# Local attention inside a four-stage kernel: weights scaled on VectorE and turned by transposes, small products spread over more steps

## The reference

```
g  = groupnorm(x)                       (groups of 3 channels over all pixels)
l  = layernorm(g) over the 96 channels of a pixel, times lg, plus lb
n  = g scaled to unit length over the 96 channels of a pixel
for each pixel q, over the keys k with |dy| <= 7 and |dx| <= 7 inside the image:
    s[k]  = n[q] . n[k]                 (-1e9 outside the window)
    w     = softmax over the 8 largest s[k], 0 elsewhere
    a[q]  = sum of w[k] * g[k]
t  = l + a
out = x + t + w2 relu(w1 t + b1) + b2
```

## Time and profile before

| | us |
|---|---|
| median of 3 runs | 18,090.14 |
| the profiled execution | 18,087.81 |
| its span | 18,086.0 |
| busy: TensorE, VectorE, ScalarE, GpSimd | 14,292.3, 15,507.5, 11,827.0, 12,383.2 |
| stage `local`: first to last instruction | 10719 to 11677 |
| its loop over tiles | 10820.5 to 11661.6 |
| TensorE's mean granted clock, whole span | 0.906 |

### The profile page before, as it was taken

One profiled execution on the slowest core, in us unless ns is written; L12 is line 12 of the kernel. 1 busy time (PEld: TensorE's weight loads), 2 busy tenths in 40 slices (PEclk: granted clock), 3 DMA queues, 4 the chain that ended last, 5 costly groups with the idle time before them and its releaser, 6 DMA issues. The chain is left out here.

```text
span 18086.0 us, 184332 instructions
## 1 busy us (share of the span) xinstructions
PE 14292.3 (79%) x38972; PEld 5918.2 (33%) x38972; DVE 15507.5 (86%) x20601; ACT 11827.0 (65%) x24107; POOL 12383.2 (68%) x5929
## 2 busy tenths in 40 slices
PE   7998878888888868888888868767777767777776
PEld 2222233333333323333333325423333233333333
DVE  6666489999999979999999964489999958999996
ACT  3555556667777636767677734378888827888882
POOL 0000079999999939999999941179988806998881
PEclk9999899999999989999999977788888888888888
DMA  1000033333333323333333321122222212222220
GB/s 27 13 18 11 12 93 107 106 107 107 107 107 106 102 77 106 108 106 107 107 106 107 106 78 37 37 67 81 82 79 79 78 29 72 81 81 79 79 80 29
DMA packets 542714, 1404.62 MB, mean 78 GB/s; under 512 B 135503, under 2 KB 191863, under 8 KB 538599
## 3 DMA queue, kind: packets, MB, share of 16 engines
q1 hardware_dynamic: 541586, 1392.84, 27.0%
HBM read 1311.24 MB, written 58.30 MB: 76 GB/s over the span
## 5 line engine op out<-in xcount | busy, mean ns | idle before, releaser
L996 PE MATMUL PS<-Hc,ident 128*128 128x448 f32 x16128 | 7494.1, 598 | 1950.8 <-POOL Hc L1308 1596.6
L1300 POOL TENSOR_TENSOR Tr<-du,BC 128x1344 f32<-128x1344 f32 x2688 | 8161.1, 3036 | 60.7 <-DVE du L1179 60.5
L996 PEld LDWEIGHTS PS<-Hc,ident 128*128 128x128 f32 x16128 | 3106.2, 205 | 6212.5 <-POOL Hc L1308 2579.3
L1118 ACT ACTIVATE PS<-dl,A 128x448 f32<-128x448 f32 x5376 | 3403.3, 633 | 2049.9 <-DVE Hr L1226 1248.6
L1308 POOL TENSOR_TENSOR Hc<-Hr,BC 128x448 f32<-128x448 f32 (+1 forms) x2688 | 3892.6, 1448 | 1030.1 <-DVE Hr L1226 947.2
L1226 DVE TENSOR_TENSOR_SCAN PS<-PS,st,Tr 128x448 f32<-128x448 f32 x3072 | 3358.2, 1135 | 142.8 <-ACT st L1132 140.6
L1233 DVE TENSOR_TENSOR Hc<-PS,BC 128x448 f32<-128x448 f32 x4480 | 2564.0, 605 | 0.0
L1126 ACT ACTIVATE PS<-cs,lneps,A 128x448 f32<-128x448 f32 x2688 | 1941.0, 722 | 175.2 <-DVE PS L1226 171.6
L719 POOL MEMSET pad<- 128x348 f32 x6 | 2.3, 387 | 2800.6 <-POOLq L67 2800.6
L1209 DVE SCALAR_TENSOR_TENSOR PS<-PS,Tr 128x448 f32<-128x448 f32 x2688 | 1644.2, 612 | 225.0 <-ACT PS L1126 214.0
L1118 ACT ACTIVATE Ar<-dl,A 128x448 f32<-128x448 f32 x2688 | 1765.5, 657 | 0.0
(11 more groups left out here) (254 smaller groups left out, 16125.1 us busy)
## 6 DMA issues: line engine op xcount, KB each, us to landing
BC<-bcscratch SPq DMA_DIRECT2D x5376, 224.0 KB, 3.6
zscratch<-zst SPq DMA_DIRECT2D x84, 224.0 KB, 2.0
bcscratch<-rows SPq DMA_DIRECT2D x336, 56.0 KB, 2.9
z<-zscratch SPq DMA_DIRECT2D x28, 672.0 KB, 4.5
xg<-mid SPq DMA_DIRECT2D x12, 1176.0 KB, 8.3
xr<-mid SPq DMA_DIRECT2D x56, 168.0 KB, 2.6
rl<-rows SPq DMA_DIRECT2D x56, 168.0 KB, 3.5
Q<-part SPq DMA_DIRECT2D x72, 98.0 KB, 4.4
```

The lines of the kernel that those rows point to most:

```text
L996: e.matmul(PS[:, YB + c, 0:T], K["ident"][:], Hc[:, g % NHC, c, :], start=False, stop=(nn == 15)).then_inc(y_done, 1)
L1118: e.activation(decay_at(u), dl[:, q % 2, c, :], ACT.Exp, scale=A[:, q // NT, c, nn:nn + 1]).then_inc(a_done, 1)
L1300: e.tensor_tensor(Tr[:, g % NTR], du[:, q % 2], b, ALU.mult).then_inc(t_done, 1)
```

## The change

In the stage `local` only:

- The diagonal matrix and ScalarE's `diagonal` go. VectorE multiplies E by one over the sum (`scale`, in place, a new instruction between `negate` and the `match_replace`, which becomes `replace`), and `turn` on TensorE is a transpose with the identity.
- `bias` moves from the end of VectorE's step to just behind `mask_`, one step later. `output` becomes two calls, one product in each of two steps.
- The small products of the next image stand in steps 4 to 14 (before: 9 to 16), about two of three steps for each kind. Each kind has its own pair of semaphores; for image one each kind also has a bank of its own (7, 5, 6), for the others all share bank 7 as before. `mean`, `total`, `normal` and the roots fall into earlier steps.
- `add`, `query` and `similar` wait for the rows of xl and xn that they read, no longer for the whole image; for image one only two of seven `scale` calls stand ahead of the loop, the rest in its first steps.
- SP loads xg ahead of the weights, the load of the next image moves from step 0 of an image to step 26 of the one before, and `bands` to steps 11 to 14.

```diff
-CENTRE, STAT, TURN = 9, 10, 9
+KINDS = {"mean": 0, "var": 0, "centre": 0, "stat": 1, "turn": 2}
+ROOTS, SCALE = 16, 18
+
+
+def spaced(s, first, n):
+
+    return next((k for k in range(n) if first + 3 * k // 2 == s), None)
 
 
 def small_products(s):
 
-    a = {4: ("mean", 0), 5: ("var", 0)}.get(s)
-    if CENTRE <= s < CENTRE + NT:
-        a = ("centre", s - CENTRE)
-    b = ("stat", s - STAT) if STAT <= s < STAT + NT else None
-    c = ("turn", s - TURN) if TURN <= s < TURN + 6 else None
+    a = {1: ("mean", 0), 2: ("var", 0)}.get(s)
+    if spaced(s, 4, NT) is not None:
+        a = ("centre", spaced(s, 4, NT))
+    b = ("stat", spaced(s, 5, NT)) if spaced(s, 5, NT) is not None else None
+    c = ("turn", spaced(s, 4, 6)) if spaced(s, 4, 6) is not None else None
     return a, b, c
 
 
...
+        def bank(b, name):
+
+            return {0: 7, 1: 5, 2: 6}[KINDS[name]] if b == 0 else 7
...
-                e.wait_ge(b7_free, order[b, what])
+                for kind in range(3):
+                    n = ahead[b, what][kind]
+                    if n and (b or kind == KINDS[name]):
+                        e.wait_ge(small_free[kind], n)
...
+                if j == 0:
+                    e.wait_ge(xn_ready, NT * b + (ys.stop - 1) // 8 + 1)
...
-                e.wait_ge(chosen, n + 1)
-                e.wait_ge(diag, n + 1)
+                e.wait_ge(scaled, n + 1)
...
                 for h, blocks in enumerate(key_blocks(i, j)):
                     for k, (_, off, kn) in enumerate(blocks):
-                        a = e.matmul(PS[0:kn, 2 + h, 112 * k:112 * k + 112], E[:, n % 2, off:off + kn], dg[:, n % 2, :],
-                                     start=True, stop=True)
+                        a = e.transpose(PS[0:kn, 2 + h, 112 * k:112 * k + 112], E[:, n % 2, off:off + kn],
+                                        K["ident"][0:112, 0:112])
                 a.then_inc(w_turned, 1)
 
             def gather(n):
...
-            def output(g):
-                e.wait_ge(hid_ready, 2 * g + 2)
-                for h in range(2):
-                    a = e.matmul(PS[0:C, 5, 0:T], w2[:, h, :], hid[:, h, :], start=(h == 0), stop=(h == 1))
-                a.then_inc(out_mm, 1)
+            def output(g, h):
+                e.wait_ge(hid_ready, 2 * g + h + 1)
+                e.matmul(PS[0:C, 5, 0:T], w2[:, h, :], hid[:, h, :], start=(h == 0), stop=(h == 1)).then_inc(out_mm, 1)
...
-            def diagonal(n):
-                s = n % 2
-                e.wait_ge(divided, n + 1)
-                if n >= 2:
-                    e.wait_ge(w_turned, n - 1)
-                e.activation(dg[:, s, :], K["ident"][0:112, 0:112], ACT.Copy, scale=den[:, s, 1:2]).then_inc(diag, 1)
...
+            def scale(n):
+                s, nk = n % 2, size(n)
+                e.wait_ge(chosen, n + 1)
+                e.wait_ge(divided, n + 1)
+                e.tensor_scalar(E[:, s, 0:nk], E[:, s, 0:nk], den[:, s, 1:2], None, ALU.mult).then_inc(scaled, 1)
+
             def negate(n):
-                s, nk = n % 2, size(n)
+                s = n % 2
                 e.wait_ge(topped, n + 1)
                 e.tensor_scalar(nb[:, s:s + 1], m8[:, s, 0:1], -1.0, None, ALU.mult).then_inc(negated, 1)
+
+            def replace(n):
+                s, nk = n % 2, size(n)
                 if n >= 2:
                     e.wait_ge(chosen, n - 1)
                 e.match_replace(R[:, s, 0:nk], m8[:, s, :], S[:, s, 0:nk], -3e9).then_inc(replaced, 1)
...
-                if i == 0 and j == 0:
-                    e.wait_ge(xl_ready, NT * (b + 1))
+                if j == 0:
+                    e.wait_ge(xl_ready, NT * b + i + 1)
...
+                if band_step(r, 10) is not None:
+                    bias(band_step(r, 10))
                 if 0 <= r - 1 < STEPS:
                     divide(r - 1)
                 if r < STEPS:
                     top(r)
-                if more and s == 4:
+                if more and s == 1:
                     mean(b + 1)
                 if 0 <= r - 1 < STEPS:
                     choose(r - 1)
                 if r < STEPS:
                     negate(r)
+                if 0 <= r - 1 < STEPS:
+                    scale(r - 1)
+                if r < STEPS:
+                    replace(r)
                 if 0 <= r - 4 < STEPS:
                     add(r - 4)
+                if more and s == 0:
+                    total(b + 1)
                 if more and s == 3:
-                    total(b + 1)
-                if more and s == 6:
                     normal(b + 1)
-                if more and s == 18:
+                if more and s == ROOTS:
                     inverted(b + 1)
-                if band_step(r, 9) is not None:
-                    bias(band_step(r, 9))
 
         def pool(e):
             def scale(b, u):
@@ -2235,37 +2261,39 @@
 
             def query(n):
                 b, i, j = tile(n)
-                if i == 0 and j == 0:
-                    e.wait_ge(xn_ready, NT * (b + 1))
+                if j == 0:
+                    e.wait_ge(xn_ready, NT * b + i + 1)
                 if n >= 4:
                     e.wait_ge(sim, n - 3)
...
-            for u in range(NT):
+            for u in range(2):
                 scale(0, u)
             for n in range(2):
                 query(n)
-            for r in range(STEPS + 13):
+            for r in range(STEPS + 14):
                 b, s = divmod(r, NTL)
-                if b + 1 < NI and 20 <= s < 20 + NT:
-                    scale(b + 1, s - 20)
+                if r + 2 < NT:
+                    scale(0, r + 2)
+                if b + 1 < NI and SCALE <= s < SCALE + NT:
+                    scale(b + 1, s - SCALE)
                 if r + 2 < STEPS:
                     query(r + 2)
-                if band_step(r, 9) is not None:
-                    finish(band_step(r, 9))
+                if band_step(r, 10) is not None:
+                    finish(band_step(r, 10))
...
+            load(0)
             for k in W:
                 e.dma_start(W[k][:], D[k]).then_inc(w_ld, 16)
-            load(0)
             for u in range(NT):
                 row(0, u)
             fold(0)
@@ -2326,25 +2354,26 @@
             for u in range(NT):
                 spread(0, u)
             bands(0, range(4))
-            for r in range(STEPS + 14):
+            load(1)
+            for r in range(STEPS + 15):
                 b, s = divmod(r, NTL)
                 if b + 1 < NI:
-                    if s == 0:
-                        load(b + 1)
-                    if STAT <= s < STAT + NT:
-                        row(b + 1, s - STAT)
-                    if s == 17:
+                    if spaced(s, 5, NT) is not None:
+                        row(b + 1, spaced(s, 5, NT))
+                    if s in (11, 12, 13, 14):
+                        bands(b + 1, [s - 11])
+                    if s == ROOTS - 1:
                         fold(b + 1)
-                    if s == 19:
+                    if s == SCALE - 1:
                         unfold(b + 1)
-                    if 19 <= s < 19 + NT:
-                        spread(b + 1, s - 19)
-                    if s in (20, 22, 24, 26):
-                        bands(b + 1, [(s - 20) // 2])
-                if band_step(r, 4) is not None:
-                    rest(band_step(r, 4))
-                if band_step(r, 10) is not None:
-                    store(band_step(r, 10))
+                    if SCALE - 1 <= s < SCALE - 1 + NT:
+                        spread(b + 1, s - SCALE + 1)
+                if b + 2 < NI and s == 26:
+                    load(b + 2)
+                if band_step(r, 5) is not None:
+                    rest(band_step(r, 5))
+                if band_step(r, 11) is not None:
+                    store(band_step(r, 11))
             for i in range(2):
                 e.wait_ge(y_out[i], 16 * len(range(i, 7 * NI, 2)))
```

More of the change, by code:

```diff
@@ L1829, in local @@
     PS = chip.PS
-    order = {}
+    order, ahead, counts = {}, {}, [0, 0, 0]
     for b in range(NI):
@@ L1834, in local @@
                 if what:
-                    order[b, what] = len(order)
+                    kind = KINDS[what[0]]
+                    ahead[b, what] = list(counts)
+                    order[b, what] = counts[kind]
+                    counts[kind] += 1
     with ExitStack() as ctx:
@@ L1857, in local @@
         gn_dve, gn_act = sems("gn_dve"), sems("gn_act")
-        b7_full, b7_free = sems("b7_full"), sems("b7_free")
+        small_full, small_free = ([sems(f"{n}_{kind}") for kind in range(3)] for n in ("small_full", "small_free"))
         squared, st_ld, fe_ld, q_ready = sems("squared"), sems("st_ld"), sems("fe_ld"), sems("q_ready")
@@ L1871, in local, with full, free @@
         y_out = [sems("y_out") for _ in range(2)]
+        def bank(b, name):
+            return {0: 7, 1: 5, 2: 6}[KINDS[name]] if b == 0 else 7
+        def full(name):
+            return small_full[KINDS[name]]
```

(40 more changed lines are left out.)

36 lines of the change are left out of this document (18 added, 18 removed).

## The result

The changed kernel takes 18,292.5 us (median of 4 runs, 18,284.7 to 18,300.3), the kernel before, timed beside it, 18,091.6 (4 runs): ratio 1.0112, interval 1.0094 to 1.0129, or 201 us more. The forecast, 18,233, was 59 us short, inside its range. The profiled execution took 18,284.7 us with a span of 18,282.8, 196.8 more than the profiled one of before.

A forecast was written before the change was run, and what follows sets the result against it. The prediction took a loop through TensorE and VectorE, neither full, to bound the stage, with the clock level mattering most. Terms 38 + 17 - 8 + 98 = +145 us on 18,087.8 gave 18,233 us, range 18,075 to 18,320.

The forecast's parts named there:

- scaling on VectorE: New scaling of E before replace and add, on the loop: 0.34 us a step, +38 us, ends 0 and +65.
- bias moved: bias now behind mask, ahead of add, in 28 steps: +17 us, ends 0 and 19.
- start: Before step 4: 18 us saved by early xg and three banks, mostly lost behind image two's sum: -8 us, ends -20 and +5.
- small products, outputs: TensorE's small products over steps 4 to 14, output in two steps: directly 0; small products' ends -10 and +10 us.
- transposes, direct: Turn by transposes saves TensorE some 1.2 us a step, all under VectorE's chain: direct gain 0.
- clock: Less busy TensorE in the loop: 25% of steps at full clock instead of 58%, +98 us, ends 0 and +172.
- the start gains what it saves: Rival: image two's sum doesn't hold VectorE, 18 us or more reach the loop; no chance of its own, alone turns no case.
- signs named in advance: Loop clock about 0.6, idle before gather over 250 us, scaling 0.4 us, largest low step 10.2 to 10.4 us, sum near 10820.
- Clock as before: Rival: share of loop steps at the full level stays 58%, +47 us, 18,135; chance 0.20.
- Transposes don't hold the clock: Rival: transposes don't count as TensorE busy, no loop step at the full level, +219 us, 18,307; chance 0.22.
- The clock rises: Rival: more even TensorE load holds the full level in the loop, -77 us, 18,011, at 90% 18,040; chance 0.16.

The follow-up runs named there:

- b_start: Kernel before with the changed kernel's start alone, the sum of image two's xg still behind step 3 on VectorE: 18,051.4 us, ratio 0.9989.
- a_bias_end: Changed kernel with bias back at the end of VectorE's step, behind add: 18,244.9 us, ratio 1.0086.
- b_scale_tr: Kernel before with scaling on VectorE, the turn by transposes and ScalarE's diagonal gone, schedule otherwise untouched: 18,242.5 us, ratio 1.0092.
- b_fill: Kernel before with every product of the turn issued twice, except in steps 9 to 16 of images that prepare a next one: 17,969.4 us, ratio 0.9941.
- a_twice: Changed kernel with every transpose of the turn issued twice in a row: 18,216.0 us, ratio 1.0069.

## Why the prediction was right, point by point

The stage grew by 200.7 us, forecast was +145. The direction and the mechanisms came out as forecast: the scaling stands on the path, the transposes give nothing back, the clock is the largest term. But scaling, bias and clock all came out larger than in the sum, and the time stayed inside the range because the range was wide. In the terms of the forecast's sum:

| term | forecast | the runs show |
|---|---|---|
| scaling on VectorE | +38 | +50 (0.45 us a step) |
| bias moved | +17 | +27 (1.02 to 1.67 us in a step that holds it, 5 us less in the others) |
| start | -8 | -5 |
| small products, outputs | 0 | some 6, as much as runs of one kernel differ |
| transposes, direct | 0 | 0 |
| clock | +98 | 100 to 117, worked out; some 10 to 30 us more are placed nowhere |

*The scaling* was under-sized. The instruction takes 0.54 us at 616 elements, where my line through L2114 gives 0.50, and it brings 0.05 us more between `negate` and `replace`. Beside GpSimd it takes longer, up to 1.21 us.

*The bias* missed by 10 us, and here a part of the mechanism was missing. I priced the instruction that moved and not what it releases: `finish` on GpSimd, which used to run at a step's end, now runs beside `choose`, and pushes `query` or `scale` beside the scaling. The prediction asked who waits for what stood behind `bias` on its own engine, but not whom its successor disturbs.

*The start* went as forecast in its mechanism: the sum of image two starts at 10816.96 (I had 10820 and 10822) and steps 1 to 3 stand behind it. That they took the 13 us I had given them, from the sum's end at 10820.38 to 10833.76, is in part luck. VectorE waits 3.8 us for ScalarE in them and not 1.5:

```profile
10825.45 0.16 DVE L2169 RECIPROCAL den<-den 112x1 f32<-112x1 f32 x1 [2.01 <-ACT e L2065]
...
10829.83 0.16 DVE L2169 RECIPROCAL den<-den 112x1 f32<-112x1 f32 x1 [1.78 <-ACT e L2065]
```

and its own work in these narrow steps, with no `add` among it yet, is some 2.6 us each and not 3.3. The two errors cancel. `b_start` shows the other case, the rival "the start gains what it saves": with the sum behind step 3 the mask of step 4 comes 17.8 us sooner, counted from the stage's first DMA, the 18 us that I had worked out as saved, and not 5.

*Small products* in other steps, and `output` in two: `a_bias_end` has all of the change but the bias's place, and its loop is 980 us against 974 of `b_scale_tr`, which has neither. So they cost some 6 us in the loop, from one profiled execution of each.

*The clock* was right in mechanism and, by the first of two countings, nearly in size. A clock of 0.76 over 809 us of loop is 52% of the time at the full level; at some 6.8 us a step that is 62 of its 107 steps. For 0.60 over 1016 us it is 20% of the time, 203 us, at some 7.2 us a step 28 steps, 26%; I had said 25%. Counted step by step from the trace's clock records, each step by its share of time at the full level, it is 61 steps before and 21 in the changed kernel, 20%. The stretches bear out the split, too. Windows of the changed kernel, steps 4 to 14 of images one, two and three, each followed by the 17 steps up to the next step 4:

```profile
10833.76:10931.34 97.58, 83.05 (x294) 47.04 (x295) 40.07 (x102) 35.45 (x86) 4.42 (x12) 0.66 0.11 26
10931.34:11093.09 161.75, 114.03 (x359) 71.78 (x358) 67.22 (x163) 42.01 (x98) 26.07 (x35) 0.55 0.13 34
11093.09:11195.12 102.03, 81.69 (x304) 45.65 (x304) 42.15 (x103) 36.82 (x88) 7.33 (x14) 0.73 0.12 29
11195.12:11356.26 161.14, 114.08 (x359) 71.56 (x358) 67.22 (x164) 42.00 (x98) 26.12 (x35) 0.53 0.13 33
11356.26:11457.25 100.99, 79.94 (x304) 44.72 (x304) 42.15 (x102) 36.48 (x88) 7.33 (x14) 0.75 0.12 29
```

With small products 0.66 to 0.75 (half the time at the full level would be 0.75), without them 0.53 to 0.55. What I under-sized is the gap between the levels. I took 2.64 us a step from two groups of four steps, and the low one ended where the clock was rising already. Four steps at the pure low level take 40.17 us in `a_bias_end` (9.94, 10.42, 10.15, 9.66), 38.3 without the scaling's four times 0.45 to 0.5; four at the full level in `b_fill` 26.6 (5.73, 6.95, 6.82, 7.10). That is 2.9 us a step: 34 steps fewer at the full level make 100 us, and the 40 of the second counting 117. Outside the stretch from mask to `add` the loop grew by 124 us (207, less 83 in that stretch), and the table leaves 129 for the clock if everything unplaced is given to it. The 12 to 29 us between stay open; the 6 of the small products are among them.

The four differences between the kernels, one change after another, make up the whole growth of the loop window, as they must: scaling with products +98 (clock 0.76 to 0.70), transposes +67 (to 0.60), start, small products and outputs +6, bias +36: the 207 us. What they tell is the share of each.

Of the signs named in advance these came: the clock at 0.60, 263 us of idling before `gather`, the sum near 10820, and 10.15 us for a low step of the largest window without `bias`. Two did not: the scaling takes 0.53 us and not 0.4, and a low step of the largest window with `bias` takes 11.46 us and not up to 10.4.

*The rivals.* "Clock as before" would have kept 0.76; it is 0.60. "Transposes don't hold the clock" is refuted by `a_twice`. "The clock rises" had the right lever on the wrong side: the clock does rise, and the kernel gains, where TensorE's gaps are filled, which this change does the opposite of.

## What to carry to other kernels

Where TensorE and another engine take turns, TensorE's idle time is not free: taking instructions away from it where it only waits can cost more than the work put on the other engine (67 us against 50 here). Before such a trade, look at the granted clock stretch by stretch, and try the reverse: TensorE work that ends before the wait does, even work that nobody needs. And when an instruction is moved, price what it releases on the other engines, by what will run beside it there.

## What the runs showed of the hardware

- Redundant work bought time: 917 more TensorE instructions and 101 us less loop (`b_fill`), with the granted clock at 0.95 instead of 0.76. That TensorE's idle time is what held the kernel before between the two levels follows from this; the work of the other engines was left as it was.
- fp32 transposes raise the clock as products do (0.70 with twice the transposes, 0.68 with products, 0.60 with single transposes).
- VectorE's `choose` takes 1.02 us instead of 0.62 while GpSimd adds two tensors, but the `top` in front of it, which reads one tensor, keeps its 0.78. The Trainium skill, "GPSIMD Engine Reference" (1. Specifications), says that GpSimd shares its SBUF interfaces with VectorE, with contention for instructions with two SBUF inputs or in a 2-port mode. The rows agree: `choose` reads R and E. The scaling, which reads one tensor, lost time too: 0.57 us for 462 elements beside the copies of `query` and 1.21 beside `scale`, where it takes 0.46 undisturbed. Whether it runs in a 2-port mode no row shows.
